# Two-layer cross-attention and mixture-of-experts on one core: the attention results are turned back into the bank of the values' products, and three turns change places in TensorE's program

## The reference, cut to what matters

```
x = x + attn0(layernorm(x), ctx)     # windows of 128 tokens: 128 queries see 128 keys
x = x + experts0(layernorm(x))
x = x + attn1(layernorm(x), ctx)     # 256 queries see the 256 keys of their sequence
x = x + experts1(layernorm(x))
# in both: softmax(q k / 4) v for each head, then the output projection wo
```

## Time and profile before

| | us |
|---|---|
| median of 3 runs (lowest to highest) | 953.57 (952.93 to 957.27) |
| the profiled execution's own time | 952.44 |
| its span in the trace | 950.5 |
| PE busy in the span | 793.5 (83%) |
| DVE busy | 610.0 (64%) |
| ACT busy | 382.6 (40%) |
| scores of a step, PE L659 | 768 matmuls in all, 217 ns each at the median |
| exponentials, ACT L1056 | 96, 1026 ns each |
| copies of the turned attention, ACT L1071, layer 0 | 15, 380 ns each |
| reductions, DVE L1316 | 180, 684 ns each |

### The profile page before, as it was taken

One profiled execution on the slowest core, in us unless ns is written; L12 is line 12 of the kernel. 1 busy time (PEld: TensorE's weight loads), 2 busy tenths in 40 slices (PEclk: granted clock), 3 DMA queues, 4 the chain that ended last, 5 costly groups with the idle time before them and its releaser, 6 DMA issues.

```text
span 950.5 us, 23219 instructions
## 1 busy us (share of the span) xinstructions
PE 793.5 (83%) x8478; PEld 596.2 (63%) x8479; DVE 610.0 (64%) x1397; ACT 382.6 (40%) x750; POOL 235.5 (25%) x203
## 2 busy tenths in 40 slices
PE   5988997897897999987869999874029999999993
PEld 3545564654556888864525666563019999999992
DVE  3546777466745766759565888676975665556561
ACT  3425556342322322222324556655324444444440
POOL 1100000100014777742100000020033544444431
PEclk9986999798999999998976999875559999999996
DMA  9966402244324333339625320167332333333334
GB/s 267 103 75 92 140 7 68 89 133 133 102 65 143 103 99 105 99 114 186 74 38 75 71 91 3 46 231 284 110 122 47 72 71 71 73 67 67 72 65 111
DMA packets 72973, 94.66 MB, mean 100 GB/s; under 512 B 14320, under 2 KB 58224, under 8 KB 72880
## 3 DMA queue, kind: packets, MB, share of 16 engines
q1 hardware_dynamic: 57088, 62.17, 27.6%
q0 software_dynamic: 13872, 29.24, 12.4%
q10 hardware_dynamic: 1952, 2.39, 0.7%
HBM read 63.09 MB, written 19.92 MB: 87 GB/s over the span
## 4 chain that ended last, share of the span: by engine, by line
PE 60%; DVE 16%; issue 6%; DMA 4%; ACT 3%; POOL 1%; POOLq 0%; DVEq 0%; SPq 0%; ACTq 0%
PE bank L879 16%; PE bank L892 13%; PE bank L672 5%; PE bank L693 4%; PE bank L798 3%; DVE arena L1606 3%; PE bank L641 3%; PE bank L864 2%; PE bank L749 2%; DVE neg_max L1316 2%; PE bank L659 2%; PE bank L787 2%; PE bank L790 2%; PE bank L687 1%; DMA sum_d<-arena,put_i 1%
## 5 line engine op out<-in xcount | busy, mean ns | idle before, releaser
L879 PE MATMUL bank<-arena 128*128 128x128 f16 x3024 | 303.8, 221 | 14.5 <-DVE arena L1611 12.5
L892 PE MATMUL bank<-arena 128*128 x1224 | 282.9, 275 | 4.7 <-DVE arena L1619 2.9
L879 PEld LDWEIGHTS bank<-arena 128*128 x3024 | 264.7, 99 | 31.5 <-issue 15.4
L1760 POOL DMA_INDIRECT arena<-xn_d,get_i x87 | 92.1, 1059 | 210.7 <-DVE arena L1606 100.1
L1184 ACT ACTIVATE arena<-bank,arena 128x128 f32<-128x128 f32 x312 | 86.4, 376 | 125.7 <-DMA arena<-in_exp_b 67.3
L1316 DVE TENSOR_REDUCE neg_max<-bank 128x2 f32<-128x512 f32 (+1 forms) x180 | 117.3, 684 | 28.7 <-PE bank L641 27.8
L892 PEld LDWEIGHTS bank<-arena 128*128 128x128 f16 x1224 | 120.2, 98 | 15.9 <-issue 13.1
L1056 ACT ACTIVATE arena<-bank 128x1024 f32<-128x1024 f32 x96 | 96.5, 1026 | 15.4 <-PE bank L659 15.0
L1770 POOL DMA_INDIRECT sum_d<-arena,put_i x39 | 63.3, 1622 | 111.9 <-DVE arena L1632 101.5
L1619 DVE TENSOR_TENSOR arena<-arena 128x512 f16<-128x512 f32 (+1 forms) x126 | 74.7, 593 | 4.3
L1744 POOL DMA_DIRECT2D xn_d<-arena x8 | 6.7, 840 | 276.4 <-DVE arena L1385 276.4
(11 more groups left out here) (185 smaller groups left out, 1129.4 us busy)
## 6 DMA issues: line engine op xcount, KB each, us to landing
arena<-arena SPq DMA_DIRECT2D x96, 128.0 KB, 5.2
arena<-in_exp_up SPq DMA_DIRECT2D x16, 512.0 KB, 3.7
arena<-in_exp_dn SPq DMA_DIRECT2D x6, 1024.0 KB, 6.4
arena<-in_exp_up SPq DMA_DIRECT2D x5, 1024.0 KB, 6.0
arena<-in_exp_b SPq DMA_DIRECT2D x39, 128.0 KB, 3.0
arena<-in_ctxT SPq DMA_DIRECT2D x8, 512.0 KB, 7.2
arena<-in_exp_dn SPq DMA_DIRECT2D x16, 256.0 KB, 4.0
xn_d<-arena POOLq DMA_DIRECT2D x8, 512.0 KB, 5.8
```

What stands on the lines that cost most here:

```text
L879: last = mm(upP[u][:, m // (UB // 2), m % (UB // 2) * P:(m % (UB // 2) + 1) * P], weights(e, 0, w, k * UPW[l] + m * P, P), rowsT[u][x][:, ...
L892: last = mm(yP[u], hidT[u][x][:, k], weights(e, 1, w, k * D, D), start=n == 0, stop=n == n_second - 1)
L1760: pool.indirect_dma_start(rows[i % 2], None, xn_d[l], bass.IndirectOffsetOnAxis(ap=get_i[:, i:i + 1], axis=0)).then_inc(s["rows_in"][i % 2 ...
```

## The change

`turn_back` writes into `attP`, bank 6, in place of `misc`, and waits only for `att_raw`. `divide` reads `attP`, and the first half of `values`, which writes that bank next, now waits for `divide` (norm_done) in place of raw_ready. The waits for x_att and nm_ready move to `turn_attention`. The first scores of a step stand ahead of `turn_maxima`. `turn_attention` stands behind the first half of the values in layer 0, and in layer 1 behind all four score parts, ahead of the values. `copy_attention` follows the last exponential of a step (in layer 0 that is where it was; in layer 1 it was behind the third of four).

```diff
--- before.py
+++ after.py
@@ -662,7 +662,7 @@
 
                 def values(i, u, half):
                     if half == 0:
-                        after(pe, s["raw_ready"], i)
+                        after(pe, s["norm_done"], i)
                     pe.wait_ge(s["exp_done"], i * NP + (half + 1) * KW)
                     for hh in range(8):
                         h = half * 8 + hh
@@ -675,14 +675,14 @@
 
                 def turn_back(i):
                     pe.wait_ge(s["raw_ready"], i + 1)
+                    for g in range(4):
+                        last = tr(attP[:, g * P:(g + 1) * P], att_raw[:, g * P:(g + 1) * P], ident)
+                    last.then_inc(s["ott_mm"], 1)
+
+                def turn_attention(i):
+                    pe.wait_ge(s["norm_done"], i + 1)
                     after(pe, s["x_att"], i)
                     pe.wait_ge(s["nm_ready"], least(i + 3, T))
-                    for g in range(4):
-                        last = tr(misc[:, g * P:(g + 1) * P], att_raw[:, g * P:(g + 1) * P], ident)
-                    last.then_inc(s["ott_mm"], 1)
-
-                def turn_attention(i):
-                    pe.wait_ge(s["norm_done"], i + 1)
                     for k in range(KD):
                         last = tr(misc[:, k * P:(k + 1) * P], att[:, k * P:(k + 1) * P], ident)
                     last.then_inc(s["at_mm"], 1)
@@ -695,17 +695,19 @@
 
                 def step(i, u):
                     first, left = isinstance(i, int) and i == 0, T - 1 - i if isinstance(i, int) else T
-                    if left > 0:
-                        turn_maxima(i + 1, 1 - u)
                     for p in range(NP):
                         scores(i, p)
+                        if p == 0 and left > 0:
+                            turn_maxima(i + 1, 1 - u)
                         if left > 1:
                             maxima(i + 2, SPREAD[l][p], SPREAD[l][p + 1])
                         if p == 0 and not first:
                             turn_back(i - 1)
-                        if p == max(NP - 2, 1) and not first:
-                            turn_attention(i - 1)
+                    if l and not first:
+                        turn_attention(i - 1)
                     values(i, u, 0)
+                    if l == 0 and not first:
+                        turn_attention(i - 1)
                     if left > 1:
                         maxima(i + 2, SPREAD[l][NP], SPREAD[l][NP + 1])
                     if not first:
@@ -1054,7 +1056,7 @@
                             after(act, s["pv_mm"], 2 * (i - 1) + half + 1)
                             dst = probs[p]
                         fn(dst.rearrange("p (b w) -> p b w", b=2), sc[p % 2], ACT.Exp, scale=SCALE / AS ** 2).then_inc(s["exp_done"], 1)
-                        if p == max(NP - 2, 1) and not first:
+                        if p == NP - 1 and not first:
                             copy_attention(i - 1)
                     if isinstance(i, int) and 12 <= i < 12 + (1 if l else FIRST0):
                         cut_high(l, i - 12)
@@ -1323,7 +1325,7 @@
 
                 def divide(i):
                     dve.wait_ge(s["ott_mm"], i + 1)
-                    sums = misc.rearrange("p (h c) -> p h c", c=32)
+                    sums = attP.rearrange("p (h c) -> p h c", c=32)
                     v.reciprocal(inv_den[:], sums[:, :, HD:V1]).then_inc(s["norm_step"], 1)
                     dve.wait_ge(s["norm_step"], i + 1)
                     after(dve, s["at_mm"], i)
```

More of the change, by code:

```diff
@@ L677, in turn_back @@
                     pe.wait_ge(s["raw_ready"], i + 1)
-                    after(pe, s["x_att"], i)
-                    pe.wait_ge(s["nm_ready"], least(i + 3, T))
                     for g in range(4):
-                        last = tr(misc[:, g * P:(g + 1) * P], att_raw[:, g * P:(g + 1) * P], ident)
+                        last = tr(attP[:, g * P:(g + 1) * P], att_raw[:, g * P:(g + 1) * P], ident)
                     last.then_inc(s["ott_mm"], 1)
@@ L685, in turn_attention @@
                     pe.wait_ge(s["norm_done"], i + 1)
+                    after(pe, s["x_att"], i)
+                    pe.wait_ge(s["nm_ready"], least(i + 3, T))
                     for k in range(KD):
```

## The result

| | before | after |
|---|---|---|
| median, same chip (executions) | 954.66 (4) | 970.23 (4) |
| lowest to highest | 952.93 to 957.27 | 962.60 to 970.61 |
| ratio after / before | | 1.0158 [1.0104, 1.0211] |
| profiled execution: time, span | 952.44, 950.5 | 970.48, 968.5 |
| its mean granted clock | 0.904 | 0.894 |

What follows compares the result with a forecast made beforehand. Both attentions were taken to hang on PE's program order and its waits. Layer 0 at +3.8 and layer 1 at +3.7 summed to +7.5 us: profiled 952.44 becomes 959.9, median 961.1, range 954.0 to 967.5.

Steps and rivals of the forecast that it cites:

- layer 0, eleven steady steps: Layer 0, steps 2 to 12: each loses 0.28 us, 0.23 from projection waiting for the copy, 0.05 from a later reduction; +3.1.
- layer 0, steps 13 to 15: Last steps of layer 0's attention: step 13 unchanged, step 14 -0.2 us, step 15 +0.6 us; +0.4.
- layer 1, eleven steady steps: Layer 1's attention: fourth scores wait for an exponential, values start later; 0.38 us a step (between 0.28 and 0.48), +4.2.
- layer 1, step 13: Layer 1: work fills PE's idle time, 0.5 us won; clock stays at 2.4 GHz, another 2.2; -2.7.
- layer 1, steps 14 and 15 to the last projection: End of layer 1's attention: the copy the projection waits for comes one exponential later, 0.94 us, twice; +1.9.
- first steps: Step 1 of each layer's attention: +0.3 us each.
- time at 1.2 GHz elsewhere: Slow-clock time outside step 13 of layer 1: the forecast sum added 0 us for it.
- Layer 0, first half: Steady step up to PE's release after divide: removed x_res wait spent on another shape change; reduction 0.05 us later (0 to 0.17).
- In steady steps neither was the last one: Turn-back in both layers: dropping its waits for x_att and nm_ready wins nothing, as other waits end later.
- Layer 0, second half: Steady step from R, PE's release after divide, to the projection: 1.49 us in place of 1.26, +0.23.
- The filled stalls pay: Rival, chance 0.17: moved work fills PE's idle 0.50 and 0.57 us a step after divide; total 951.0 us, not slower.
- The clock elsewhere: Rival, chance 0.05: slow stretches shift at stage ends, 2.2 to 2.4 us each; one less gives 958.8, two less 956.5.

Runs made afterwards that it cites:

- A: Edit: turn-back into bank 6 with its waits. Alone in both layers against the kernel before: 984.62 us, ratio 1.0005, layer 0 step 5.38 us.
- B: Edit: scores ahead of the turned maxima. Alone in both layers against the kernel before: 993.15 us, ratio 1.0090.
- e6_b: Kernel before with only the scores ahead of the turned maxima, both layers, turn-back still to bank 7: 993.15 us, ratio 1.0090; steps 5.54 and 7.65 us.
- e1_ab: Changed kernel without the moves of turned attention and its copy; bank 6 and scores first stay: 986.05 us, ratio 1.0017 to before; steps 5.26 and 7.65.
- e3_c1: Kernel before with only layer 1's turned attention behind the fourth scores, its copy behind the fourth exponential: 994.97 us, ratio 1.0101; layer 1 step 7.915.
- C0: Edit: layer 0's turned attention behind the first half of the values. Alone against the kernel before: 990.22 us, ratio 1.0061, layer 0 step 5.33 us.
- f1_bank: Kernel before with turn-back into bank 6 in both layers and scores first in layer 0 only: 954.62 us, ratio 0.9972; repeated 983.94 us, 0.9975.
- y_before: Kernel before, unchanged, run again as a second sample on chip 0: 984.88 us, ratio 1.0009.

## Why the prediction came out as it did, point by point

| term | forecast | measured |
|---|---|---|
| layer 0, eleven steady steps | +3.1 (0.28 each) | +1.0 (0.09) |
| layer 0, steps 13 to 15 | +0.4 | +1.0 (23.01 to 24.05) |
| layer 1, eleven steady steps | +4.2 (0.38) | +5.2 (0.475) |
| layer 1, step 13 | -2.7 | -0.6 (11.03 to 10.45) |
| layer 1, steps 14 and 15 to the last projection | +1.9 | +0.8 |
| first steps | +0.6 | 6.38 to 7.43 and 8.17 to 12.90, not told apart from the clock |
| sum | +7.5 | +7.4; at equal clock +6.3, +6.3, +7.9 |
| time at 1.2 GHz elsewhere | 0 | 182.5 to 205.3 us, at 0.3 some +6.8 |

- **Direction: right, and so is the mechanism of the later turned attention in both layers.** The steps carry the loss, on three chips and in the first trace. That they add up to +7.4, where +7.5 was forecast, is luck: the errors cancel, in layer 0 down, in layer 1 and its step 13 up.
- **Layer 0, first half: wrong.** "Between 0 and 0.17 I take 0.05": the reduction came 0.12 earlier. A bound of zero excluded a gain, and A with B is one. "In steady steps neither was the last one" is the step that failed here: the 0.17 at 108.62, read as the price of a change of shape, was PE waiting for `keep_maxima` (0.11 behind its end, in before and in e6_b alike). So A wins something, and the transition behind the scores cost 0.10 where I took 0.17. The Trainium skill, page "TensorEngine Tiling (Array Packing)", section Key Properties, says that changing the tiling mode drains TensorE. Here the gap from the row-tiled scores to the turned maxima, which load all 128 rows, was 0.10, so what that change costs fits into 0.10. The gaps between two shapes' loads were 0.10 to 0.12, 0.17, 0.21 and 0.33 by the pair of shapes.
- **Layer 0, second half: right.** R to projection 1.49 was forecast, 1.55 and 1.47 came.
- **Layer 1, steady: right in kind, too small.** The working gave 8.02 for 7.59, +0.43, with a slip of 0.15; the forecast then took 0.38, the middle of its bounds. Measured is 0.475. The slip was smaller than taken (0.105, e1_ab), and the fourth scores ahead of the turned attention dearer: 0.37 by themselves (e3_c1), where the working had 0.28. From the fourth scores to the turned attention it took 0.67 (588.40 to 589.07) and 0.76 in the next step, not 0.55.
- **"The filled stalls pay": no in the changed kernel,** yes in C0 alone.
- **Step 13: the step that failed first.** The longest idle time there came down from 1.98 to 1.39, as forecast (1.4). But "I expect that the clock stays at 2.4 GHz, another 2.2": it fell in all four traces of the changed kernel (3, 10, 3 and 3 us at 1.2 GHz), and in two of the four of before it didn't fall at all, although the same 1.98 us of idle time stands there. From the projection in step 12 to the last one of layer 1 the four traces of before take 29.4 in the mean (27.9 to 30.8), those of the changed kernel 31.6 (31.0 to 33.3): +2.2, not -0.8. In layer 0 too the changed kernel has 3 us at 1.2 GHz in step 13 or 14 that three of four traces of before don't have.
- **"The clock elsewhere", 0.05: the step by which the number missed.** I let the clock move by one or two stretches of 2.2 to 2.4 us of cost. The time at 1.2 GHz differs between executions of one program by far more, and one profiled execution of before, at 182.5 us, said nothing of its spread. The first measurement of the changed kernel had 205 in three of four executions, and so at its median; at 0.3 us each, 22.8 us more are worth some 6.8 of the 8.1 us that the forecast was short. That is an estimate, for of before only the profiled execution's clock is known. Not all of it fits: the changed kernel's one execution at 182.5 us took 962.60, 10.2 above the profiled execution of before at the same 182.5, where the later sets have 6.3 to 7.9; and of the 18.0 us between the two profiled executions, 7.4 and 6.8 leave 3.8 open.
- **Open:** whether the change itself raises the time at 1.2 GHz. In the three later measurements its means are 188.3, 183.8 and 187.8 us against 186.5, 181.6 and 182.7 for all executions of before beside them: each higher, by 1.8, 2.2 and 5.1, about the standard error of such a difference (1.9 to 4.5). 205 in three of four wasn't met again. Against all executions of before in each of the three, the medians are +7.6, +7.0 and +9.6 us; so 961 to 964 is what these would give, and 970 what was measured first. The edits by themselves don't settle it either: three kernels with parts of the change had 13 to 15 us more at 1.2 GHz than before on chip 3, and two sets of one program differed by 10.5.
- **A better version?** f1_bank comes out 0.28% [0.9946, 0.9998] and 0.25% [0.9943, 1.0006] under before, with a step of layer 0 shorter by 0.17 in both traces, eleven times 1.9 us. An identical copy of before came out 0.57% under in the same set, so the traces show the gain and the medians don't yet.

## What to carry to other kernels

Before an order is changed to fill a stall, look at what the moved work must wait for after the change: C0 fills the stall at R only as long as the values don't themselves wait for `divide`, and B wins only when the bank behind it is free. Price each pair of edits, not each edit, where they share a bank or a stall. A small gap that a row puts down to "issue" can still be a wait: hold its start against the ends of all that the instruction waits for. And read the time at 1.2 GHz of every execution before two medians are compared: here it moved a median by up to 6 us, nearly as much as the change.

## What the runs showed of the hardware that I had not expected

- Of one program, the kernel before, single executions had between 153.7 and 208.4 us at 1.2 GHz, both in one measurement on chip 3; they took 974.62 and 994.32 us.
- Sets of twelve and 35 executions of the same program on one chip had medians 6.0 us apart, with an interval of the ratio, 0.9914 to 0.9973, that didn't allow for it.
- The same idle time of 1.98 us on PE was followed by 7 us at 1.2 GHz in two traces and by none in two.
- Chips 0 and 3 took about 30 us longer with every kernel than chip 5 and the chip of the first measurement. y_before loses it against before between about 305 and 420 us, in the experts of layer 0, where the DMAs moved 77 to 80 GB/s in place of 92 to 101, for the same program. Why isn't known.
